# A transformer block with adaptive norm and FP4 quantisers on one core: the scaling of q, two quantiser steps and the row statistics change engine or form, and every order is written anew

## The chip, the cores and the metric

The kernel runs on one core of one Trainium2 chip. The metric is the device time of one execution in microseconds (us). A core has TensorE (PE in the profile; PEld is its weight load), VectorE (DVE), ScalarE (ACT), GpSimd (POOL) and SyncE (SP), which here only issues DMAs. Each engine works through its own list of instructions in order, and the engines wait for each other by semaphores.

## What is computed

There are 32 batches of 256 tokens with 128 features, all float32. Cut to what matters:

```
mod = silu(c) @ wmod                     # six vectors per batch: sa, ca, ga, sb, cb, gb
h = layernorm(x) * (1 + ca) + sa
q, k, v = h @ Wq + bq, ...               # each reshaped to (16 heads, 8, 256)
attn = softmax(k^T v * temperature)      # per head 256 x 256, over the last axis
x = x + ga * (q @ attn)
h = layernorm(x) * (1 + cb) + sb
hid = silu(fp4(h) @ fp4(w_gate).T) * (fp4(h) @ fp4(w_up).T)      # 352 wide
x = x + gb * (fp4(hid) @ fp4(w_down).T)
```

`fp4` quantises blocks of 16 elements: the block's largest magnitude over 6 is the scale, the scaled values are rounded to the grid 0, 0.5, 1, 1.5, 2, 3, 4, 6 and scaled back. With two rows of tokens on each partition, a batch's `h` is 128 x 256 and its `hid` 128 x 704.

## The kernel before

The work is a software pipeline over the batches. Each engine has a function `step(k)` that is called once per step; it names tasks with a lag, and `at(k, 3, maxes, 7)` means that in step k the engine does part 7 of the task `maxes` for batch k - 3. So the order on each engine is written out by hand, task by task, and one step of every engine finishes one batch.

One batch passes through these tasks. `stats1` and `var1` (VectorE: two `bn_stats`, one for each row, two `bn_aggr`, then a variance plus epsilon and a negated mean), `rstd1_pow` and `normalise1` (GpSimd), `x_transpose` (TensorE), `h_out` (ScalarE), `kv_proj` and `q_proj` (TensorE). `k_hi`, `v_hi`, `k_lo`, `v_lo` (VectorE) split k and v into two parts for the fast matmul format; SyncE stores the parts to `split_dram` (`store_split`, eight DMAs a batch) and loads them back in another layout (`load_stacks`, five DMAs). `scores` (TensorE) writes one head's scores into one of the four slots of `score_ps`; `maxes` (VectorE, eight a batch) reads two heads at a time; `exps` (ScalarE, 32 a batch) writes `probs` and the row sums. `row_sums_inv` (VectorE) inverts the sums, `q_out` (ScalarE) copies q out of PSUM into `q_T`, and `q_scaled` (GpSimd) multiplies it by the inverses into `q_z`. `mix` (TensorE) contracts q with the probabilities, `gate1` (VectorE) makes `gated`, `residual1` (GpSimd) makes `x1`.

Then comes the second norm, in the same form as the first (`stats2` to `shift2`), and the two quantisers, of `h2` and of `hid`. Each is: `max`, `scale`, `recip` (VectorE), `y` (GpSimd: value times the reciprocal scale), `exponent` and `magic` (VectorE), `add`, `sub`, `rescale` (GpSimd). `magic` turns the exponent of a value into the number that, added and taken away again, rounds it:

```
def magic(mag):
    return nc.vector.tensor_scalar(mag[:, :], mag[:, :], 1.5, MAGIC, ALU.max, ALU.mult)
```

Between the quantisers stand `gate_proj`, `up_proj`, `tanh`, `silu` and `times_up`, behind them `hid_transpose`, `hidT_out`, `down_proj`, `gate2` (VectorE, makes `ffn_g`), `residual2` and the store. The weights are quantised once, in one piece of 1120 columns, by `ff_weights_max` and `ff_weights_magic` (VectorE), `ff_weights_scaled` and `ff_weights_rounded` (GpSimd), in steps 2 and 3.

Four further PSUM banks are shared by the matmul outputs; `wait_bank` holds a matmul until the readers of the bank's last contents are done.

Of the kernel before, what the change touches and what calls it, by code (L numbers as in the profile page):

```python
# [15 lines left out]
FF = 352  # L16
# [12 lines left out]
STAGES = 10  # L29
# [3 lines left out]
def adaln_block(nc, x, wq, bq, wk, bk, wv, bv, temperature, w_gate, w_up, w_down, c, wmod, out):  # L33
    with ExitStack() as ctx:
# [11 lines left out]
        w_q = sb("w_q", [128, D])  # L46
        w_kv = sb("w_kv", [128, 2, D])
# [4 lines left out]
        minus_half = sb("minus_half", [128, 2])  # L52
# [25 lines left out]
        hT = sb("hT", [128, T])  # L78
# [53 lines left out]
        qT_ps_made, qT_made = sem("qT_ps_made"), sem("qT_made")  # L132
# [15 lines left out]
        ff_zeroed, ff_fp4 = sem("ff_zeroed"), sem("ff_fp4")  # L148
        ff_ps_made, ff_T_made = sem("ff_ps_made"), sem("ff_T_made")
# [43 lines left out]

        @block.sync
        def _(sp):
            sp.dma_start(c_rows[:, :], c).then_inc(c_in, 16)
            sp.dma_start(w_mod[:, :], wmod).then_inc(wmod_in, 16)
# [6 lines left out]
            def load_later():  # L204
# [4 lines left out]
            def load_ff():  # L209
                for i, w in enumerate((w_gate, w_up)):  # L210
                    for t, n in enumerate(FT):
                        sp.dma_start(w_ff[0:n, (3 * i + t) * D:(3 * i + t + 1) * D],
                                     w[128 * t:128 * t + n, :]).then_inc(ff_rows_in, 16)
                sp.dma_start(w_ff[:, 6 * D:NW], w_down).then_inc(ff_rows_in, 16)

            def load_mod(b, c):
                if b == 0:
                    sp.wait_ge(mod_step, 6)
                    sp.dma_start(mod_dram, mod_rows[:, :, :].rearrange("b n f -> b (n f)"))\
                        .then_inc(mod_stored, 16)  # L220
                    sp.wait_ge(mod_stored, 16)
# [28 lines left out]
            def load_stacks(b, c):  # L250
                p = c % 2
                if b < 2:
                    sp.wait_ge(k_zeroed[b], 1)
                wait_dma(sp, split_stored, b, STORES * 16)
                wait_batches(sp, scored, b - 1, H)
                sp.dma_start(v_stack[p][:, :, :].bitcast(F32),
                             split_dram[p, 1].rearrange("g r s j n -> (r s j) g n")).then_inc(stack_loaded[p], 16)
                for r in range(R):
# [32 lines left out]
        def _(pool):  # L291
# [134 lines left out]
            def step(k):  # L426
# [17 lines left out]
                if k == 1:  # L444
                    zero_q()
# [611 lines left out]
```

## Time and profile before

| what | value |
|---|---|
| median of 3 runs | 664.52 us (663.1 to 665.88) |
| the profiled execution's own time | 663.56 us |
| its span, first to last instruction | 661.8 us |
| mean granted TensorE clock | 0.949 of full speed |
| DVE busy | 589.0 us (89%) |
| ACT busy | 566.7 us (86%) |
| PE busy | 550.2 us (83%) |
| POOL busy | 515.0 us (78%) |

The busy shares are means over three parts: a start in which the first batches fill the pipeline, a long even part, and a drain of the last batches. The profiled execution's time stands 1.8 us above its span; that is what lies around the instructions.

### The profile page before, as it was taken

The numbers are of one execution on the slowest core, as the hardware profiler recorded it, in microseconds if no ns is written. First come the engines' busy times: TensorE is split into PE (matmuls) and PEld (weight loads), VectorE is DVE, ScalarE is ACT, GpSimd is POOL, SyncE is SP. The second block draws the span as 40 slices with busy tenths as digits, with TensorE's granted clock in tenths as the row PEclk, the third lists the DMA queues.
The fourth block names the chain that finished last, engine by engine and source line by source line (L and its number), as shares of the span: only waits on it lengthen the run. The fifth ranks groups of instructions, "written<-read, shape, count | busy, mean of one in ns | idle before, by whom it ended". The sixth has DMA issues, their size and how long they took to land.

```text
span 661.8 us, 15572 instructions
## 1 busy us (share of the span) xinstructions
PE 550.2 (83%) x4336; PEld 372.4 (56%) x4336; DVE 589.0 (89%) x1331; ACT 566.7 (86%) x2281; POOL 515.0 (78%) x655
## 2 busy tenths in 40 slices
PE   4468688889999988888888898998888999987773
PEld 2345365666665665566666665665566666654343
DVE  5578489999999999999999999999999999998551
ACT  2289599999999999999999999999999999999111
POOL 2105747888888898988888888888888888877884
PEclk9568799999999999999999999999999999999866
DMA  4656525555566555566555566554556655550000
GB/s 117 160 139 152 137 73 152 136 135 135 156 160 160 136 140 132 141 161 157 145 145 143 145 161 160 151 145 134 141 135 160 160 140 135 136 144 9 10 8 25
DMA packets 87873, 86.14 MB, mean 130 GB/s; under 512 B 8550, under 2 KB 83532, under 8 KB 87788
## 3 DMA queue, kind: packets, MB, share of 16 engines
q1 hardware_dynamic: 87344, 84.94, 49.6%
q8 instruction: 37, 0.61, 0.4%
q14 instruction: 48, 0.39, 0.2%
q10 hardware_dynamic: 444, 0.20, 0.1%
HBM read 47.29 MB, written 37.81 MB: 129 GB/s over the span
## 4 chain that ended last, share of the span: by engine, by line
POOL 36%; DVE 27%; issue 19%; PE 8%; ACT 4%; DMA 2%; SPq 2%; POOLq 1%; DVEq 1%; ACTq 1%
DVE neg_max L638 8%; POOL hid_q L400 7%; POOL hid_q L404 6%; POOL rstd L322 4%; POOL h_c L329 4%; DVE hid L753 3%; DVE hid_am L604 3%; POOL h_c L335 3%; POOL h L342 3%; POOL q_z L355 3%; ACT probs L491 3%; PE bank L935 3%; POOL h_q L375 2%; DVE stats L704 2%; PE score_ps L893 2%
## 5 line engine op out<-in xcount | busy, mean ns | idle before, releaser
L491 ACT ACTIVATE probs<-score_ps,neg_max 128x256 f32<-128x256 f32 x1024 | 472.8, 491 | 22.3 <-DVE neg_max L638 19.8
L638 DVE TENSOR_REDUCE neg_max<-score_ps 128x4 f32<-128x1024 f32 x256 | 308.2, 1204 | 16.5 <-PE score_ps L893 15.9
L893 PE MATMUL score_ps<-v_stack,k_stack 128*128 128x256 f32 x1024 | 212.1, 324 | 48.4 <-DMA k_stack<-split_dram 30.6
L491 ACT ACTIVATION_READ_ACCUMULATOR probs<-score_ps,neg_max 128x1 f32 x1024 | 228.6, 223 | 0.0
L893 PEld LDWEIGHTS score_ps<-v_stack,k_stack 128*128 128x128 f32 x1024 | 148.7, 194 | 118.6 <-ACT probs L491 65.6
L935 PE MATMUL bank<-probs,q_z 128*32 128x256 f32 x2048 | 140.0, 393 | 12.3 <-POOL q_z L355 12.3
L935 PEld LDWEIGHTS bank<-probs,q_z 128*32 128x32 f32 x2048 | 54.5, 111 | 66.9 <-POOL q_z L355 29.9
L955 PE MATMUL bank<-wgu_T,h_T 128*128 128x352 f32 x128 | 52.6, 495 | 18.0 <-issue 17.9
L984 PE MATMUL bank<-wd_T,hid_T 118*128 118x128 f32 x384 | 58.0, 290 | 5.9 <-ACT hid_T L525 5.6
L984 PEld LDWEIGHTS bank<-wd_T,hid_T 118*128 118x128 f32 x384 | 50.4, 199 | 11.7 <-ACT hid_T L525 11.0
L404 POOL TENSOR_TENSOR hid_q<-hid_q,hid_mag 128x704 f32<-128x704 f32 x32 | 53.9, 1685 | 2.5
L400 POOL TENSOR_TENSOR hid_q<-hid_q,hid_mag 128x704 f32<-128x704 f32 x32 | 54.0, 1686 | 2.4 <-DVE hid_mag L615 2.4
L309 POOL TENSOR_TENSOR rstd<-ve,minus_half 128x2 f32<-128x2 f32 x32 | 23.5, 736 | 41.2 <-DVE nm L659 21.9
L525 ACT ACTIVATE hid_T<-bank 118x384 f32<-118x384 f32 x64 | 34.1, 534 | 22.1 <-PE bank L975 21.9
L322 POOL TENSOR_TENSOR rstd<-ve,minus_half 128x2 f32<-128x2 f32 x32 | 30.7, 959 | 28.0 <-DVE nm L718 26.3
L964 PE MATMUL bank<-wgu_T,h_T 128*128 128x352 f32 x128 | 50.5, 482 | 0.5 <-DVE kv_lo L683 0.5
L363 POOL TENSOR_TENSOR x<-gated,x_in 128x256 f32<-128x256 f32 x32 | 23.3, 727 | 30.0 <-DVE gated L696 29.9
L382 POOL TENSOR_TENSOR hid_q<-hid,hid_rs 128x704 f32<-128x704 f32 x32 | 44.5, 1390 | 1.5 <-DVE hid_rs L769 1.3
L409 POOL TENSOR_TENSOR hid_q<-hid_q,hid_sc 128x704 f32<-128x704 f32 x32 | 44.4, 1388 | 0.2
L913 PE MATMUL bank<-w_kv,hT 128*128 128x256 f32 x128 | 41.4, 417 | 1.3 <-ACT hT L501 1.3
L519 ACT ACTIVATE tanh_g<-bank 128x352 f32<-128x352 f32 x64 | 30.2, 472 | 14.0 <-PE bank L955 13.0
L355 POOL TENSOR_TENSOR q_z<-q_T,inv_sum 128x128 f32<-128x128 f32 x64 | 25.1, 415 | 21.1 <-DVE inv_sum L690 21.1
(104 smaller groups left out, 904.0 us busy)
## 6 DMA issues: line engine op xcount, KB each, us to landing
split_dram<-kv_hi SPq DMA_DIRECT2D x128, 128.0 KB, 2.4
split_dram<-kv_lo SPq DMA_DIRECT2D x128, 128.0 KB, 2.4
v_stack<-split_dram SPq DMA_DIRECT2D x32, 512.0 KB, 4.2
k_stack<-split_dram SPq DMA_DIRECT2D x128, 128.0 KB, 4.6
mod_bc<-mod_dram SPq DMA_DIRECT2D x32, 256.0 KB, 5.1
x_in<-in_L_attn_x_dram SPq DMA_DIRECT2D x32, 128.0 KB, 2.5
out_dram<-out_t SPq DMA_DIRECT2D x32, 128.0 KB, 2.1
w_mod<-in_L_wmod_dram SPq DMA_DIRECT2D x1, 384.0 KB, 4.0
```

What stands on the lines that cost most here:

```text
L322: nc.gpsimd.tensor_tensor(rstd2[:, :], ve2[:, :], minus_half[:, :], ALU.pow).then_inc(rstd2_made, 1)
L355: nc.gpsimd.tensor_tensor(dst, q_T[:, c, a, :].rearrange("p (g r j) -> p g r j", g=G, r=R), inv_sum[:, :, a].rearrange("p (g r) -> p g r", ...
L382: nc.gpsimd.tensor_tensor(blocks16(hid_q[:, :], 2 * FF), blocks16(hid[:, :], 2 * FF), spread16(hid_rs[:, :], 2 * FF), ALU.mult).then_inc(h ...
L400: nc.gpsimd.tensor_tensor(hid_q[:, :], hid_q[:, :], hid_mag[:, :], ALU.add).then_inc(hid_t_made, 1)
L404: nc.gpsimd.tensor_tensor(hid_q[:, :], hid_q[:, :], hid_mag[:, :], ALU.subtract)\
L491: nc.scalar.activation(probs[p][:, h, a, :], score_ps[:, h % 4, a, :], ACT.Exp, bias=neg_max[:, p, n:n + 1], accum_out=row_sum[:, p, h, a: ...
L638: nc.vector.tensor_reduce(neg_max[:, p, 4 * u:4 * u + 4], score_ps[:, lo:lo + 2, :, :].rearrange("p b a n -> p (b a) n"), AX.X, ALU.max, n ...
L893: last = nc.tensor.matmul(score_ps[:, h % 4, a, :], k_stack[p][:, h, 128 * a:128 * a + 128], v_stack[p][:, h // R, :], start=True, stop=True)
L935: last = nc.tensor.matmul(bank_mix[32 * g:32 * g + 32, 0:T], q_z[p][:, a, g, r, :], probs[p][:, R * g + r, a, :], start=(i == 0), stop=(i ...
L955: nc.tensor.matmul(bank_gate[a][:, 0:FF], h2_T[:, 128 * a:128 * a + 128], wgu_T[:, 0, :], start=True, stop=True).then_inc(gate_ps_made[a], 1)
L964: nc.tensor.matmul(bank_up[a][:, 0:FF], h2_T[:, 128 * a:128 * a + 128], wgu_T[:, 1, :], start=True, stop=True).then_inc(up_ps_made[a], 1)
L984: last = nc.tensor.matmul(bank_down[:, a * D:(a + 1) * D], hid_T[:, a, t, :], wd_T[:, t, :], start=(t == 0), stop=(t == HT - 1))
```

## The change

On VectorE, `q_scaled` now reads q straight from its PSUM bank, so `q_out` and the tile `q_T` are gone, and `q_proj` moves to the step of the mixing. The row statistics take both rows in one `bn_stats` over interleaved elements; the constant for epsilon stands ready in the tile, a small `tensor_reduce` adds the pairs, another negates the means, and the factor that this form leaves is folded into `mod_T` and `mod_rows`. On GpSimd, `scale` and `magic` of both quantisers are added and `q_scaled` is gone. The weights are quantised in three pieces. ScalarE's queue takes part of the first two batches' stores and loads. `hT` has four buffers, the banks are shared out anew, and all five orders are new (with 14 instead of 10 stages, since the lags are counted in another way).

```diff
-        bank_xT, bank_kv, bank_q, bank_h2T, bank_mix, bank_down = bank_1, bank_3, bank_0, bank_0, bank_2, bank_1
-        bank_gate, bank_up, bank_hidT = (bank_2, bank_1), (bank_3, bank_0), (bank_0, bank_2)
+        bank_xT, bank_kv, bank_q, bank_h2T, bank_mix, bank_down = bank_0, bank_0, bank_2, bank_3, bank_2, bank_1
+        bank_gate, bank_up, bank_hidT = (bank_2, bank_3), (bank_0, bank_3), (bank_0, bank_2)
...
     # gpsimd
-            def q_scaled(b, c):
...
+            def block_scale(sc, am, tiny):
+                return nc.gpsimd.tensor_scalar(sc, am, NUDGE / 6.0, tiny, ALU.mult, ALU.max)
...
+            def magic(mag):
+                return nc.gpsimd.tensor_scalar(mag[:, :], mag[:, :], 1.5, MAGIC, ALU.max, ALU.mult)
+
+            def h2_magic(b, c):
+                pool.wait_ge(h2_z_made, b + 1)
+                magic(h2_mag).then_inc(h2_mag_made, 1)
...
     # scalar
-            def q_out(b, c):
-                wait_batches(act, qT_ps_made, b + 1)
-                wait_batches(act, qz_made, b - 3, 2)
-                nc.scalar.activation(q_T[:, c, :, :], halves(bank_q[:, 0:T]), ACT.Copy).then_inc(qT_made, 1)
...
     # vector
+            def variance(var, stats, p):
+
+                full = stats[:, p, 2:6]
+                pairs = bass.AP(tensor=full.tensor, offset=full.offset, ap=[list(full.ap[0]), [3, 2], [4, 2]])
+                return nc.vector.tensor_reduce(var[:, :], pairs, AX.X, ALU.add)
+
+            def minus_mean(nm, stats, p):
+                return nc.vector.tensor_reduce(nm[:, :], stats[:, p, 1:6:3].unsqueeze(2), AX.X, ALU.max, negate=True)
...
-                for a in range(2):
-                    nc.vector.bn_stats(stats1[:, a, :], x_in[:, b % NX, a, :]).then_inc(stat_a, 1)
...
+                nc.vector.bn_stats(stats1[:, c % 2, 0:6], by_row(x_in[:, b % NX, :, :])).then_inc(stats1_made, 1)
...
+            def q_scaled(b, c):
...
+                for a in range(2):
+                    dst = diagonal(q_z[p][:, a, :, :, :].rearrange("p g r j -> p g (r j)"))
+                    last = nc.vector.tensor_tensor(
+                        dst, bank_q[:, a * 128:(a + 1) * 128].rearrange("p (g r j) -> p g r j", g=G, r=R),
+                        inv_sum[:, :, a].rearrange("p (g r) -> p g r", g=G).unsqueeze(3)
+                        .to_broadcast([128, G, R, DH]), ALU.mult)
...
     # tensor
             def q_proj(b, c):
                 wait_batches(pe, hT_made, b + 1)
-                wait_bank(b, [(h2T_made, b - 3)], (hidT_made[0], b - 5), (hid_made[1], b - 4), (qT_made, b))
+                wait_bank(b, [(silu_made[0], b - 1)], (hidT_made[1], b - 3), (gated_made, b), (qz_made, b))
...
-                at(k, 1, q_proj)
+                at(k, 6, q_proj)
```

Three places of the new orders follow; in each row stand the line, the operation and the tiles.

VectorE, one piece of a step in the even part, from the score maximum ahead of the second norm's statistics to the next maximum. Before:

```order
L638 TENSOR_REDUCE neg_max<-score_ps 128x4
L704 BN_STATS stats<-x 128x6 x2
L666 TENSOR_SCALAR kv_hi<-bank,temp 128x256
L711 BN_AGGR mv<-stats 128x2 x2
L611 TENSOR_SCALAR hid_mag<-hid_q 128x704
L717 TENSOR_SCALAR ve<-mv 128x2
L718 TENSOR_SCALAR nm<-mv 128x2
L615 TENSOR_SCALAR hid_mag<-hid_mag 128x704
L638 TENSOR_REDUCE neg_max<-score_ps 128x4
```

And now:

```order
L753 TENSOR_REDUCE neg_max<-score_ps 128x4
L838 BN_STATS stats<-x 128x6
L761 TENSOR_REDUCE var<-stats 128x2
L764 TENSOR_REDUCE nm<-stats 128x2
L761 TENSOR_REDUCE var<-stats 128x2
L764 TENSOR_REDUCE nm<-stats 128x2
L753 TENSOR_REDUCE neg_max<-score_ps 128x4
```

The two norms' small steps stand together, the split of k has moved behind the next maximum with `exponent` of `hid`, and `magic` has left the engine.

GpSimd, the piece of a step from the first residual to the last step of the quantiser of `hid`. Before:

```order
L363 TENSOR_TENSOR x<-gated,x_in 128x256
L382 TENSOR_TENSOR hid_q<-hid,hid_rs 128x704
L322 TENSOR_TENSOR rstd<-ve,minus_half 128x2
L329 TENSOR_SCALAR h_c<-x,nm,rstd 128x128 x2
L335 TENSOR_TENSOR h_c<-h_c,mod_bc 128x256
L342 TENSOR_TENSOR h<-h_c,mod_bc 128x256
L400 TENSOR_TENSOR hid_q<-hid_q,hid_mag 128x704
L404 TENSOR_TENSOR hid_q<-hid_q,hid_mag 128x704
L355 TENSOR_TENSOR q_z<-q_T,inv_sum 128x4x4x8 x2
```

And now:

```order
L401 TENSOR_TENSOR x<-gated,x_in 128x256
L437 TENSOR_TENSOR hid_q<-hid,hid_rs 128x704
L373 TENSOR_TENSOR rstd<-var,minus_half 128x2
L380 TENSOR_SCALAR h_c<-x,nm,rstd 128x128 x2
L387 TENSOR_TENSOR h_c<-h_c,mod_bc 128x256
L441 TENSOR_SCALAR hid_mag<-hid_mag 128x704
L394 TENSOR_TENSOR h<-h_c,mod_bc 128x256
L466 TENSOR_TENSOR hid_q<-hid_q,hid_mag 128x704
L411 TENSOR_SCALAR h_sc<-h_am 128x16
L470 TENSOR_TENSOR hid_q<-hid_q,hid_mag 128x704
L430 TENSOR_TENSOR h_q<-h,h_rs 128x256
L475 TENSOR_TENSOR hid_q<-hid_q,hid_sc 128x704
```

`magic` of `hid` and `scale` of `h2` (L411) have come in between steps that were neighbours, and the scaling of q is gone; `magic` of `h2` and `scale` of `hid` stand a little further on.

SyncE's queue for the first batch's split parts and their loads. Before:

```order
L229 DMA split_dram<-kv_hi 16x8x256 x2
L229 DMA split_dram<-kv_lo 16x8x256 x2
L229 DMA split_dram<-kv_hi 16x8x256 x2
L201 DMA x_in<-in_L_attn_x_dram 128x256
L229 DMA split_dram<-kv_lo 16x8x256 x2
L256 DMA v_stack<-split_dram 128x4x256
L260 DMA k_stack<-split_dram 32x4x256 x4
```

And now:

```order
L205 DMA split_dram<-kv_hi 16x8x256 x2
L205 DMA split_dram<-kv_lo 16x8x256 x2
L230 DMA v_stack<-split_dram 128x4x256
L240 DMA k_stack<-split_dram 32x4x256 x2
L251 DMA x_in<-in_L_attn_x_dram 128x256
```

The other four stores and two loads stand in ScalarE's queue, and the load of x has moved behind.

## Rows read from the trace of the kernel before

**Rows 1.** The page: its span, and its busy time by engine

```profile
span 661.8 us, 15572 instructions
...
PE 550.2 (83%) x4336; PEld 372.4 (56%) x4336; DVE 589.0 (89%) x1331; ACT 566.7 (86%) x2281; POOL 515.0 (78%) x655
```

**Rows 2.** Windows: busy us of each engine in a stretch of the even part

```profile
core 0: us, PE busy (x) PEld busy (x) DVE busy (x) ACT busy (x) POOL busy (x), PEclk, DMA share, GB/s
...
200.00:300.00 100.00, 90.02 (x770) 61.08 (x770) 98.76 (x228) 97.53 (x397) 87.55 (x113) 1.00 0.57 150
```

**Rows 3.** Timeline of DVE: `gated` of the first, second and last batch

```profile
59.65 0.41 DVE L696 TENSOR_TENSOR gated<-bank,mod_bc 128x256 f32<-128x256 f32 x1
...
83.00 0.41 DVE L696 TENSOR_TENSOR gated<-bank,mod_bc 128x256 f32<-128x256 f32 x1
...
621.22 0.42 DVE L696 TENSOR_TENSOR gated<-bank,mod_bc 128x256 f32<-128x256 f32 x1 [0.92 <-PE bank L935]
```

**Rows 4.** Groups of DVE by form: busy us, mean ns of one, idle before

```profile
L604 DVE TENSOR_REDUCE hid_am<-hid 128x44 f32<-128x704 f32 x32 | 28.0, 874 | 0.3
...
L615 DVE TENSOR_SCALAR hid_mag<-hid_mag 128x704 f32<-128x704 f32 x32 | 16.6, 520 | 0.1
...
L645 DVE BATCH_NORM_STATS2 stats<-x_in 128x6 f32<-128x128 f32 x64 | 15.2, 278 | 0.0
...
L604 DVE TENSOR_REDUCE h_am<-h 128x16 f32<-128x256 f32 x32 | 13.4, 419 | 11.3 <-POOL h L342 10.8
L696 DVE TENSOR_TENSOR gated<-bank,mod_bc 128x256 f32<-128x256 f32 x32 | 13.4, 418 | 0.9 <-PE bank L935 0.9
...
L615 DVE TENSOR_SCALAR h_mag<-h_mag 128x256 f32<-128x256 f32 x32 | 9.2, 287 | 0.2
...
L608 DVE TENSOR_SCALAR h_sc<-h_am 128x16 f32<-128x16 f32 x32 | 8.0, 250 | 0.0
...
L652 DVE BATCH_NORM_AGGREGATE mv<-stats 128x2 f32<-128x6 f32 x64 | 7.6, 160 | 0.0
...
L608 DVE TENSOR_SCALAR hid_sc<-hid_am 128x44 f32<-128x44 f32 x32 | 6.4, 200 | 0.1
...
L658 DVE TENSOR_SCALAR ve<-mv 128x2 f32<-128x2 f32 x32 | 6.2, 195 | 0.0
```

**Rows 5.** Timeline of DVE in the even part: start us, us, instruction

```profile
249.15 0.52 DVE L615 TENSOR_SCALAR hid_mag<-hid_mag 128x704 f32<-128x704 f32 x1
249.59 1.21 DVE L638 TENSOR_REDUCE neg_max<-score_ps 128x4 f32<-128x1024 f32 x1
```

**Rows 6.** Groups of POOL and ACT by form: busy us, mean ns of one

```profile
L400 POOL TENSOR_TENSOR hid_q<-hid_q,hid_mag 128x704 f32<-128x704 f32 x32 | 54.0, 1686 | 2.4 <-DVE hid_mag L615 2.4
...
L316 POOL TENSOR_SCALAR xn<-x_in,nm,rstd 128x128 f32<-128x128 f32 x64 | 28.9, 462 | 0.4
...
L355 POOL TENSOR_TENSOR q_z<-q_T,inv_sum 128x128 f32<-128x128 f32 x64 | 25.1, 415 | 21.1 <-DVE inv_sum L690 21.1
...
L507 ACT ACTIVATE q_T<-bank 128x256 f32<-128x256 f32 x32 | 12.7, 395 | 16.3 <-PE bank L926 16.2
...
L297 POOL MEMSET b_pad<- 128x384 f32 x1 | 0.4, 418 | 0.0
```

**Rows 7.** Timeline near the end: `h_sc` on DVE beside a POOL instruction

```profile
612.02 1.68 POOL L400 TENSOR_TENSOR hid_q<-hid_q,hid_mag 128x704 f32<-128x704 f32 x1
...
612.76 0.96 DVE L608 TENSOR_SCALAR h_sc<-h_am 128x16 f32<-128x16 f32 x1
```

**Rows 8.** Timeline of DVE at the start: first score maximum, and a long wait

```profile
29.15 1.22 DVE L638 TENSOR_REDUCE neg_max<-score_ps 128x4 f32<-128x1024 f32 x1 [6.78 <-PE score_ps L893]
...
77.53 0.29 DVE L611 TENSOR_SCALAR h_mag<-h_q 128x256 int32<-128x256 int32 x1 [7.64 <-POOL h_q L375]
```

**Rows 9.** Timeline of SP's queue: first batch's first stores, last loads

```profile
13.40 1.20 SPq L229 DMA_DIRECT2D split_dram<-kv_hi  x2
...
21.37 1.93 SPq L260 DMA_DIRECT2D k_stack<-split_dram  x4
```

More of the change, by code:

```diff
@@ L1 @@
+import math
 from contextlib import ExitStack
@@ L21 @@
 NW = 2 * 3 * D + FF
+FFC = (slice(0, 3 * D), slice(3 * D, 6 * D), slice(6 * D, NW))
+FFB = tuple(slice(s.start // QB, s.stop // QB) for s in FFC)
 EPS = 1e-5
@@ L250, in load_stacks @@
-            def load_stacks(b, c):
[L251 to L258, printed above, removed]
-                    rows = slice(32 * r, 32 * r + 32)
-                    sp.dma_start(k_stack[p][rows, r:H:R, :].bitcast(F32),
-                                 split_dram[p, 0, :, r].rearrange("g s j n -> (s j) g n"))\
-                        .then_inc(stack_loaded[p], 16)
+                if b >= 2:
+                    store_v_hi_on(sp, b, c)
@@ L483, in exps, with store_v_hi, store_v_lo, load_k_stack @@
+            def store_v_hi(b, c):
+                if b < 2:
+                    store_v_hi_on(act, b, c)
+            def store_v_lo(b, c):
+                if b < 2:
+                    store_v_lo_on(act, b, c)
+            def load_k_stack(b, c):
+                if b < 2:
+                    for r in range(R // 2, R):
+                        load_k_stack_on(act, b, c, r)
             def exps(b, c, h):
@@ L593, in gates @@
                 nc.vector.tensor_copy(mod_rows[:, 1, :], rows[:, 1, :]).then_inc(mod_step, 1)
-                nc.vector.tensor_scalar(mod_rows[:, 2, :], rows[:, 2, :], 1.0, None, ALU.add).then_inc(mod_step, 1)
+                nc.vector.tensor_scalar(mod_rows[:, 2, :], rows[:, 2, :], 1.0, ROOT_D, ALU.add, ALU.mult).then_inc(mod_step, 1)
                 dve.wait_ge(mod_step, 4)
@@ new lines, in step @@
+                at(k, 10, hid_recip)
+                at(k, 7, maxes, 5)
+                if k == 5:
+                    ff_recip(0)
+                at(k, 8, stats2_rows)
+                at(k, 8, variance2)
+                at(k, 4, variance1)
+                if k == 6:
+                    ff_recip(2)
+                at(k, 7, maxes, 6)
+                at(k, 5, v_hi)
+                at(k, 5, k_hi)
+                if k == 3:
+                    ff_recip(1)
+                at(k, 10, hid_exponent)
@@ new lines, in step @@
+                at(k, 7, maxes, 7)
+                at(k, 5, v_lo)
+                at(k, 5, k_lo)
+                at(k, 9, silu, 0)
+                at(k, 6, maxes, 0)
+                if k == 4:
+                    shift_and_scale()
+                at(k, 8, h2_max)
+                if k == 4:
+                    biases()
+                at(k, 7, row_sums_inv)
+                at(k, 9, silu, 1)
+                at(k, 8, h2_recip)
+                at(k, 6, maxes, 1)
+                if k == 6:
+                    ff_exponent(0)
@@ new lines, in step @@
+                if k == 5:
+                    zero_k(0)
+                if k == 4:
+                    ff_exponent(1)
+                at(k, 7, q_scaled)
+                if k == 6:
+                    ff_exponent(2)
+                if k == 5:
+                    ff_magic(1)
+                if k == 4:
+                    ff_max(0)
+                if k == 5:
+                    ff_max(2)
+                if k == 0:
+                    ff_max(1)
+                at(k, 9, times_up, 0)
```

732 lines of the change are left out of this document (395 added, 337 removed).

## The prediction

> **What bounds the kernel now.** I read the page's busy line first, then a stretch of the even part, then single starts.
>
> The busy line [rows 1] only says that four engines are close: DVE 589.0, ACT 566.7, PE 550.2, POOL 515.0 of a span of 661.8 us. The stretch [rows 2] says more: in 100 us DVE works 98.76, ACT 97.53, PE 90.02, POOL 87.55. So VectorE sets the pace there, ScalarE stands just behind it, and GpSimd has slack.
>
> The pace itself comes from the starts of `gated` [rows 3]: second batch 83.00, last 621.22, so 538.22 us for 30 steps, 17.94 us a step. In one step DVE works 17.72 and waits 0.22, ACT works 17.50, POOL 15.71. What is not in those 30 steps is the start, 83.0 us to the second `gated`, and the drain, 661.8 - 621.2 = 40.6 us behind the last. All sums below are 30 steps plus what start and drain change.
>
> A duration is not what an instruction costs DVE, since the next one starts before it ends: `magic` of `hid` lasts 0.52 and the next starts 0.44 behind it [rows 5]. I take 0.08 us off each duration.
>
> **DVE, part by part, for one step.** Removed [rows 4]: four `bn_stats` of 128 elements (two rows of each norm; the second norm's group reads the same), 4 x (0.278 - 0.08) = 0.79. Four `bn_aggr`, 4 x 0.08 = 0.32. Four additions and negations of the mean, priced like `ve` at 0.195, 4 x 0.115 = 0.46; the trace shows most of them shorter, so I take 0.36. `scale` twice, 0.17 + 0.12 = 0.29. `magic` twice, 0.44 + 0.21 = 0.65. Together 2.41.
>
> Added: two `bn_stats` of 256. VectorE's reductions give a slope, (874 - 419) / 448 = 1.02 ns an element, so 128 more elements cost 0.13 and one costs 0.33, two 0.66. Four tiny `tensor_reduce`: the same line at nearly no elements gives 0.16, less 0.08, so 0.32. Two multiplications of q from PSUM: `gated` also reads PSUM, 0.418 for 256, so 0.29 for 128, less 0.08, and 0.42 for both. Together 1.40. Bounds for what the trace doesn't show: the interleaved `bn_stats` may cost as little as today's (0.40 for two) or the whole duration of two today's each (1.11); the split pattern of q may cost up to the whole 0.418 of `gated` twice (0.84). I take the slope, as the operations are the nearest kinds. Net: -1.01, with ends -1.27 and -0.14. DVE's work becomes 16.7.
>
> DVE also has waits. It keeps 0.22, and the two `exponent` steps, which remain, can be held by GpSimd: `h_sc` takes 0.96 instead of some 0.16 while a POOL instruction of 1.68 runs beside it, and both end at 613.7 [rows 7]. Before, ten such scalar operations a step met a GpSimd that was idle 12% of the time; now two meet one that hardly idles. I put 0.3 on it, so DVE asks for about 17.2.
>
> This is also what the Trainium skill states, SBUF — State Buffer, Who interferes with whom: VectorE in a two-port mode and GpSimd take one pair of ports as an exclusive lock, and the loser waits out the whole instruction. By that rule, the trace agrees (0.96 for a 128x16 operation), and it speaks against loading GpSimd further.
>
> **ACT.** `q_out` goes, 0.395 long [rows 6]; its neighbours overlap it, so I count two thirds, 0.26 a step, with ends 0 and 0.395. 17.50 becomes 17.2, and some of the 17.50 is waiting for maxima that the busy time hides.
>
> **GpSimd.** `q_scaled` goes, 2 x 0.415 = 0.83 [rows 6]. Two `magic` and two `scale` come. The trace has no such operation at that size. The low end is a memset's 1.09 ns an element all in: 0.77 and 0.28. The high end is the nearest operation, `xn`, 0.462 for 128 elements, taken as proportional: 2.54 and 0.92. In between lies a two-input operation, 1.69 for 704 and, on the line through 0.415 for 128, 0.70 for 256. I take `xn` for the first 128 elements and the memset's slope for the rest, since `magic` reads one tile like `xn`: 1.09 and 0.60. The two `scale` are below `xn`, 0.25 each. Sum: 15.71 - 0.83 + 1.69 + 0.50 = 17.07, and 0.2 for neighbours that wait for each other. So GpSimd asks for 17.3.
>
> The Trainium skill, GPSIMD Engine Reference, 4.1 Engine selection, calls GpSimd about half as fast as VectorE with two inputs, but roughly at line rate with one. By the first part `magic` would cost 1.69 and 0.70 and the gain of the even part would be gone; by the second it is close to the value I took. No row of this trace decides.
>
> Three engines then ask for 17.2, 17.2 and 17.3 in a step. None has slack to give another. The new order also asks for short answers: `scale` of `h2` stands on GpSimd between `add` and `sub` of `hid`, and VectorE has only an inversion and a `silu` between `max` and `recip` to cover it, so a late GpSimd shows at once as a wait of DVE. I take the longest, **17.3**: 30 x (17.3 - 17.94) = **-19.2**.
>
> **The start.** First scores: SP issues eight stores and five loads for the first batch between 13.40 and 23.30 [rows 9]. Half of the stores and two loads go to the other queue, and a load of x moves behind. Four stores at 0.6, two loads at 0.48 and the x load at 0.6 make 3.96, so the first maximum comes at about 25 instead of 29.15 [rows 8]. The new work ahead (a memset of `k_stack` now behind the split, weights in thirds) lies beside DMAs in flight. Bounds: 0, if ScalarE's queue is late by what SyncE's gains, and 5. Weights: the second `gated` comes 23.35 behind the first, 5.4 more than a step, and DVE waits 7.64 us at 77.53 for `h_q`, which stood behind the whole weight work on GpSimd [rows 3, 8]. In three pieces spread over steps with no FFN work I leave 1.4 of it, so -4.0 (ends 0 and -5.4). Start: **-8**, from 0 to -10.
>
> **The drain.** Behind the last `gated`, GpSimd takes three `hid` and one `h2` through the quantisers. For each `hid`, `magic` costs 1.09 instead of 0.52 and `scale` 0.05 more: +0.6 for two, in a chain; for the first, where GpSimd never idles, +1.3. **+2.5**, from 0 to +5.
>
> **Sum**, against the profiled execution's 663.6 (0.96 below the median of the runs shown): 663.6 - 19.2 - 8 + 2.5 = 638.9, **639**.
>
> **The rivals.**
> - *The start only.* The even part keeps its pace, 17.9: the ring of maximum, exponentials and the next scores in `score_ps`, or one of the banks (x, kv, up and hid now share one), waits longer than DVE gains. For it: ACT is at 97.53 already. Against it: `maxes` is not made longer and ACT loses 0.26. -1.2 - 8 + 2.5 gives 657. Chance 0.10.
> - *The held exponents.* Each waits half an average POOL instruction (515.0 us over 655 is 0.79 [rows 1]), 0.4 instead of 0.15: 16.7 + 0.22 + 0.8 makes DVE ask for 17.75. -5.7 - 8 + 2.5 gives 652. Chance 0.10.
> - *GpSimd at the price of two inputs.* 15.71 - 0.83 + 2.39 + 0.5 + 0.2 = 18.0 a step: +1.8 - 8 + 4 gives 661, no change. Against it: the memset's row. Chance 0.08.
> - *Slower: GpSimd becomes the bound.* `magic` at the proportional price, 2.54 + 0.92: 15.71 - 0.83 + 3.46 + 0.5 + 0.2 = 19.0. 30 x 1.1 = 33, - 8 + 5, gives 693. It decides from 18.15 a step on, since start and drain give back 3 us and 3.3 must be lost. Chance 0.10.
> - *My forecast*, 626 to 651. Chance 0.62.
>
> **How the numbers follow.** 0.5%, 3.3 us, is about what a measurement of this kernel tells from no change. The forecast's own range: at 17.0 a step, -28 - 10 + 0 gives 626; at 17.55, -11.7 - 4 + 3 gives 651. With the next two rivals at 652 and 657 it reaches 658 and holds 0.82. Faster: 0.62 + 0.10 + 0.10 = 0.82. Same: 0.08. Slower: 0.10.
>
> **What would show it.** In the profile after: `gated` at steps of 17.3, first maximum at 25, the second `gated` some 8 earlier than 83; DVE near 16.7 and POOL near 17 busy a step; `magic` on GpSimd 1.1 and 0.6; `bn_stats` 0.41; `exponent` of `hid` at most 0.3 longer than now on average. Wrong would be: `magic` above 1.7, DVE and POOL both with slack while the step stays near 17.9 (then the ring or a bank), or a first maximum later than 29.

## The result: slower by 7%, GpSimd sets the pace

The changed kernel took 712.15 us (median of 4 runs, 709.68 to 713.79) against 665.20 for the kernel before (663.1 to 668.83): a ratio of 1.0697, 95% interval 1.0639 to 1.0754. The forecast was 639, with 693 for the rival in which GpSimd becomes the bound. Its profiled execution has a span of 710.8 us.

The page of the changed kernel, its span, its busy time, and the shares of the engines in its chain of waits:

```profile
span 710.8 us, 15569 instructions
...
PE 556.7 (78%) x4336; PEld 380.9 (54%) x4336; DVE 567.8 (80%) x1084; ACT 559.8 (79%) x2249; POOL 625.3 (88%) x730
...
POOL 72%; issue 16%; ACT 4%; PE 3%; DVE 2%; DMA 2%; POOLq 1%; SPq 1%; ACTq 0%
```

The same stretch as in [rows 2], and `gated` of the second and the last batch as in [rows 3]:

```profile
200.00:300.00 100.00, 81.71 (x675) 56.90 (x675) 85.17 (x166) 86.72 (x350) 95.94 (x111) 1.00 0.48 132
```

```profile
72.10 0.41 DVE L830 TENSOR_TENSOR gated<-bank,mod_bc 128x256 f32<-128x256 f32 x1
...
662.83 0.42 DVE L830 TENSOR_TENSOR gated<-bank,mod_bc 128x256 f32<-128x256 f32 x1 [2.02 <-PE bank L1063]
```

The busy share has changed sides: GpSimd from 87.55 to 95.94, VectorE from 98.76 to 85.17. The step is (662.83 - 72.10) / 30 = 19.69 us, not 17.94: +52.5 over 30 steps. The second `gated` comes 10.9 earlier than 83.00, and the drain is 710.8 - 662.8 = 48.0 instead of 40.6, +7.4. Together +49.0, which is what the spans differ by.

The groups of GpSimd and VectorE that answer to [rows 4] and [rows 6] (mean ns of one behind the busy time; then the idle time before them and what ended it):

```profile
L441 POOL TENSOR_SCALAR hid_mag<-hid_mag 128x704 f32<-128x704 f32 x32 | 82.4, 2576 | 5.9 <-DVE hid_mag L723 3.7
L466 POOL TENSOR_TENSOR hid_q<-hid_q,hid_mag 128x704 f32<-128x704 f32 x32 | 53.8, 1680 | 0.2
...
L441 POOL TENSOR_SCALAR h_mag<-h_mag 128x256 f32<-128x256 f32 x32 | 34.6, 1081 | 5.5 <-DVE h_mag L723 3.3
L366 POOL TENSOR_SCALAR xn<-x_in,nm,rstd 128x128 f32<-128x128 f32 x64 | 28.2, 448 | 3.2
...
L411 POOL TENSOR_SCALAR hid_sc<-hid_am 128x44 f32<-128x44 f32 x32 | 11.8, 368 | 3.0 <-DVE hid_am L720 0.3
L411 POOL TENSOR_SCALAR h_sc<-h_am 128x16 f32<-128x16 f32 x32 | 8.9, 279 | 8.1 <-DVE h_am L720 5.4
```

```profile
L723 DVE TENSOR_SCALAR hid_mag<-hid_q 128x704 int32<-128x704 int32 x32 | 19.0, 593 | 4.5 <-POOL hid_q L437 4.5
...
L820 DVE TENSOR_TENSOR q_z<-bank,inv_sum 128x128 f32<-128x128 f32 x64 | 15.1, 277 | 0.0
...
L720 DVE TENSOR_REDUCE h_am<-h 128x16 f32<-128x256 f32 x32 | 13.4, 419 | 30.6 <-POOL h L394 30.6
L769 DVE BATCH_NORM_STATS2 stats<-x_in 128x6 f32<-128x256 f32 x32 | 13.4, 419 | 0.0
...
L761 DVE TENSOR_REDUCE var<-stats 128x2 f32<-128x4 f32 x64 | 9.2, 152 | 1.4 <-issue 0.2
...
L856 DVE RECIPROCAL h_rs<-h_sc 128x16 f32<-128x16 f32 x32 | 8.1, 253 | 28.9 <-POOL h_sc L411 28.9
```

One line matters most: `magic` of `hid` takes 2.58 us on GpSimd, more than `add` or `sub` with their two inputs (1.68) and five times its 0.52 on VectorE. What VectorE saved has become waiting for GpSimd: 28.9 us ahead of `h_rs` and 30.6 ahead of `h_am` (where it was 11.3 before), about 0.9 us a step each. The added VectorE operations last as long as the forecast said.

GpSimd itself hardly waits for anyone. In some 15 steps from 200 us on it pauses nine times a step, 0.08 to 0.11 us each, and only two of the 133 pauses are longer (0.48). Part of its busy time is holding by VectorE all the same: the two `normalise2` instructions take 1.25 us together where they took 0.89 before, with VectorE's `exponent` of `hid` beside the second.

```profile
271.47 1.25 POOL L380 TENSOR_SCALAR h_c<-x,nm,rstd 128x128 f32<-128x128 f32 x2
```

```profile
271.96 0.52 DVE L723 TENSOR_SCALAR hid_mag<-hid_q 128x704 int32<-128x704 int32 x1
```

In the kernel before, the `rstd` ahead of them was the one that was long, 0.97 us instead of 0.71 beside `magic` of `hid`. So only 0.1 us a step of this is new.

### The profile page after: what moved, and what is told of

Same layout as the page of the kernel before. It is cut to its first block, busy times and chain, and to the rows that moved or that the text cites. A ratio compares the mean times of both kernels' runs of the same rounds, so it can differ in the third digit from the quotient of the medians.

```text
span 710.8 us, 15569 instructions
## 1 busy us (share of the span) xinstructions
PE 556.7 (78%) x4336; PEld 380.9 (54%) x4336; DVE 567.8 (80%) x1084; ACT 559.8 (79%) x2249; POOL 625.3 (88%) x730
## 4 chain that ended last, share of the span: by engine, by line
POOL 72%; issue 16%; ACT 4%; PE 3%; DVE 2%; DMA 2%; POOLq 1%; SPq 1%; ACTq 0%
POOL hid_mag L441 12%; POOL hid_q L466 8%; POOL hid_q L470 8%; POOL hid_q L475 6%; POOL h_c L380 5%; POOL h_mag L441 5%; POOL hid_q L437 4%; ACT probs L604 3%; POOL xn L366 3%; POOL rstd L373 3%; POOL h_q L453 3%; POOL h_c L387 3%; POOL h_q L457 3%; POOL x L401 3%; POOL rstd L359 2%
## 5 line engine op out<-in xcount | busy, mean ns | idle before, releaser
L753 DVE TENSOR_REDUCE neg_max<-score_ps 128x4 f32<-128x1024 f32 x256 | 308.5, 1206 | 17.8 <-PE score_ps L1019 17.3
L1019 PE MATMUL score_ps<-v_stack,k_stack 128*128 128x256 f32 x1024 | 230.5, 327 | 44.0 <-ACT probs L604 39.3
L1019 PEld LDWEIGHTS score_ps<-v_stack,k_stack 128*128 128x128 f32 x1024 | 154.8, 194 | 135.5 <-ACT probs L604 90.0
L1063 PE MATMUL bank<-probs,q_z 128*32 128x256 f32 x2048 | 137.6, 400 | 44.1 <-DVE q_z L820 44.1
L1063 PEld LDWEIGHTS bank<-probs,q_z 128*32 128x32 f32 x2048 | 62.9, 113 | 86.9 <-DVE q_z L820 49.6
L441 POOL TENSOR_SCALAR hid_mag<-hid_mag 128x704 f32<-128x704 f32 x32 | 82.4, 2576 | 5.9 <-DVE hid_mag L723 3.7
L633 ACT ACTIVATE hid_T<-bank 118x384 f32<-118x384 f32 x64 | 32.4, 508 | 40.9 <-PE bank L1109 40.6
L1097 PE MATMUL bank<-wgu_T,h_T 128*128 128x352 f32 x128 | 51.0, 480 | 16.7 <-issue 16.7
L1109 PE MATMUL bank<-ident,hid_q 128*118 128x128 f32 x192 | 33.2, 286 | 16.2 <-POOL hid_q L475 15.6
L441 POOL TENSOR_SCALAR h_mag<-h_mag 128x256 f32<-128x256 f32 x32 | 34.6, 1081 | 5.5 <-DVE h_mag L723 3.3
L380 POOL TENSOR_SCALAR h_c<-x,nm,rstd 128x128 f32<-128x128 f32 x64 | 35.8, 567 | 3.5
L720 DVE TENSOR_REDUCE h_am<-h 128x16 f32<-128x256 f32 x32 | 13.4, 419 | 30.6 <-POOL h L394 30.6
```

What stands on the lines that cost most here:

```text
L380: nc.gpsimd.tensor_scalar(h2_c[:, a, :], x1[:, c, a, :], nm2[:, a:a + 1], rstd2[:, a:a + 1], ALU.add, ALU.mult).then_inc(h2_c_made, 1)
L441: return nc.gpsimd.tensor_scalar(mag[:, :], mag[:, :], 1.5, MAGIC, ALU.max, ALU.mult)
L753: nc.vector.tensor_reduce(neg_max[:, p, 4 * u:4 * u + 4], score_ps[:, lo:lo + 2, :, :].rearrange("p b a n -> p (b a) n"), AX.X, ALU.max, n ...
L1019: last = nc.tensor.matmul(score_ps[:, h % 4, a, :], k_stack[p][:, h, 128 * a:128 * a + 128], v_stack[p][:, h // R, :], start=True, stop=True)
L1063: last = nc.tensor.matmul(bank_mix[32 * g:32 * g + 32, 0:T], q_z[p][:, a, g, r, :], probs[p][:, R * g + r, a, :], start=(i == 0), stop=(i ...
L1097: nc.tensor.matmul(bank_up[a][:, 0:FF], h2_T[:, 128 * a:128 * a + 128], wgu_T[:, 1, :], start=True, stop=True).then_inc(up_ps_made[a], 1)
```

## The experiments

Each time has the kernel before beside it on the same chip, and the ratio is to that; steps are worked out from `gated` as above. A and B are the two theories that each expectation weighs. From the fifth run on, the base is the changed kernel with a cheap `magic` (run 5); run 7 is the kernel before with it, and runs 9 and 11 are edits of run 6.

A step is the mean over 30, and some steps near both ends are shorter than the rest. Between 200 and 500 us it is (492.45 - 210.11) / 16 = 17.65 us in run 5 where the mean is 17.49, and 17.98 before, 19.99 in the change, 18.92 in run 6, 18.30 in run 8, 17.56 in run 10 and 18.64 in run 11. Below, this is the even step, and it goes with busy shares of 200 to 500 us.

### 1. Both magics back on VectorE, all else as changed

```diff
-                at(k, 9, h2_magic)          # gpsimd
-                at(k, 10, hid_magic)
+                at(k, 9, h2_magic)          # vector, behind h2_exponent
+                at(k, 10, hid_magic)        # vector, behind hid_exponent
```

> The changed kernel with both magic steps back on VectorE, each right behind its exponent; all else as changed. Theory A (the price of magic on GpSimd, 2.58 + 1.08 us a step, is what made the step 19.7 us): GpSimd falls from about 19.7 to 16.0 a step, VectorE asks for 16.9 + 0.65 = 17.5 and sets the pace, step about 17.6; with start 72 and drain about 41 the run takes about 643 us. Rival B (the new orders, the shared banks or the handshakes of scale between the two engines cost it): the step stays at 18.5 or more and the run takes over 670 us.

Measured: 680.68 us (679.27 to 682.94), ratio 1.0229 [1.0193, 1.0266], step 18.86. Moving the magics back returns 31 of the 47 us, and GpSimd's busy share falls to 82% (200 to 500 us), but A's 643 did not come. The numbers are B's: a step of 18.5 or more, over 670 us. They don't show B's reason, since run 5 keeps the same orders, banks and scales and has a step of 17.49. VectorE is 97.6% busy here, and two of its groups show where part of the time went:

```profile
L713 DVE TENSOR_SCALAR hid_mag<-hid_q 128x704 int32<-128x704 int32 x32 | 28.3, 883 | 4.5 <-POOL hid_q L437 4.5
L717 DVE TENSOR_SCALAR hid_mag<-hid_mag 128x704 f32<-128x704 f32 x32 | 28.1, 879 | 1.1
```

`exponent` and `magic` of `hid` take 0.88 each instead of 0.50 and 0.52. In all steps from 200 to 500 us each of them begins beside a GpSimd instruction and ends 0.37 to 0.39 us behind that one's end. Runs 6, 9 and 11 look at this.

### 2. The kernel before, both magics on GpSimd alone

```diff
-                at(k, 4, h2_magic)          # vector
-                at(k, 6, hid_magic)
+                at(k, 4, h2_magic)          # gpsimd, ahead of h2_add
+                at(k, 5, hid_magic)         # gpsimd, ahead of hid_add
```

> The kernel before with one part of the change alone: both magic steps on GpSimd, ahead of their add; its own orders, banks and statistics stay. Theory A: GpSimd asks for 15.7 + 3.66 = 19.4 and some gaps, step 19.6 to 20.2, run 715 to 735 us, slower than the whole change. Rival B (the orders are the cost): the slack of GpSimd takes most of it and the run stays below 690 us.

Measured: 785.66 us (784.65 to 788.71), ratio 1.1798 [1.1756, 1.1841], step 21.86. Worse than both theories. The magics take 2.56 and 1.07 here too, but GpSimd is only 86% busy from 200 to 500 us. The waits point to its answers coming too late in the old order: TensorE's weight loads wait 103 us for `q_z`, and VectorE 95 us for `h_q`. TensorE's granted clock is 0.92 in this stretch, where it was 1.00 before, so part of the length may be TensorE's; no run separates this.

### 3. A multiplication in place of the maximum

```diff
-                return nc.gpsimd.tensor_scalar(mag[:, :], mag[:, :], 1.5, MAGIC, ALU.max, ALU.mult)
+                return nc.gpsimd.tensor_scalar(mag[:, :], mag[:, :], 1.5, MAGIC, ALU.mult, ALU.mult)
```

> The changed kernel with a multiplication in place of the maximum in magic on GpSimd (the rounding numbers come out otherwise, the work is the same). If the maximum is the dear operation: magic of hid takes 1.0 to 1.3 us instead of 2.58 and the step falls to about 18. If every operation with one input and two constants costs that: it stays at 2.58, and the run at about 712 us.

This version leaves out the floor of `magic`, so its rounding numbers and its output are wrong, and only its time is of use. Measured, one run: 635.89 us, step (592.1 - 70.3) / 30 = 17.39. One operation in each of the two magics moves the time by 76 us. The magics take 0.78 and 0.41, below the 1.0 to 1.3 that was expected of a cheap one.

### 4. GpSimd's price list

A kernel of its own that computes nothing of the block: GpSimd is the only engine that computes, and runs each form four times over 44, 128, 256 and 704 elements.

```diff
+ run(lambda: nc.gpsimd.tensor_scalar(tiles[name][:, 0:n], src[:, 0:n], 1.5, 2.0, op0, op1))
+ run(lambda: nc.gpsimd.tensor_scalar(tiles[name][:, 0:n], src[:, 0:n], 1.5, None, op0))
+ run(lambda: nc.gpsimd.tensor_scalar(tiles[name][:, 0:n], src[:, 0:n], sc[:, 0:1], sc[:, 1:2], op0, ALU.mult))
```

> Only the price list: GpSimd runs one-input operations on 44, 128, 256 and 704 elements, each waiting for the one ahead, with nothing beside it; no reference work is done and the output is zeros. Line rate (theory of my prediction): any one-input form takes about 0.2 + 0.83 ns an element, 0.8 to 1.1 us for 704. Dear maximum: forms with max take about 2.58 for 704 and 1.08 for 256, add and mult forms less than half of it. Dear second operation: two operations cost about twice one.

Measured; the groups by form, six at 704 elements and two at 128 (the tile's name is the form):

```profile
L73 POOL TENSOR_SCALAR max_mult<-src 128x704 f32<-128x704 f32 x4 | 10.2, 2558 | 0.4
...
L75 POOL TENSOR_SCALAR max_only<-src 128x704 f32<-128x704 f32 x4 | 7.9, 1972 | 0.3
L79 POOL TENSOR_TENSOR tt_add<-src 128x704 f32<-128x704 f32 x4 | 5.4, 1357 | 0.3
...
L77 POOL TENSOR_SCALAR add_mult_ptr<-src,sc 128x704 f32<-128x704 f32 x4 | 3.7, 930 | 0.4
...
L73 POOL TENSOR_SCALAR add_mult<-src 128x704 f32<-128x704 f32 x4 | 3.1, 777 | 0.3
L80 POOL COPY copy<-src 128x704 f32<-128x704 f32 x4 | 3.1, 769 | 0.3
...
L73 POOL TENSOR_SCALAR max_mult<-src 128x128 f32<-128x128 f32 x4 | 2.5, 637 | 0.4
...
L77 POOL TENSOR_SCALAR add_mult_ptr<-src,sc 128x128 f32<-128x128 f32 x4 | 1.8, 449 | 0.4
```

Two additions or multiplications cost as much as a copy. A maximum among the two makes it 3.3 times as much. No other engine computes, and SyncE's stores of the output are over long before the 704-element instructions start at 74 us, so no contention is in it. The theory that two operations cost twice one has fallen too: a single operation (1.97) is dearer than two multiplications (0.78). The form of `xn` (`add_mult_ptr`) is 0.449 at 128 elements, near the 0.462 of [rows 6], and 0.930 at 704.

### 5. The same rounding numbers by multiply and add

The maximum only has to keep the number from falling below 1.5 x 2^22. With 15/32 x 2^22 times the exponent's 1.5 x 2^e, plus 1.25 x 2^22, the number lies in the same power of two for all exponents that occur.

```diff
-                return nc.gpsimd.tensor_scalar(mag[:, :], mag[:, :], 1.5, MAGIC, ALU.max, ALU.mult)
+                return nc.gpsimd.tensor_scalar(mag[:, :], mag[:, :], MAGIC * 15 / 32, MAGIC * 1.25, ALU.mult, ALU.add)
```

> The changed kernel with the magic numbers on GpSimd made by multiply and add in place of maximum and multiply: the exponent's 1.5 x 2^e times 15/32 x 2^22, plus 1.25 x 2^22. That lies in the same power of two as the old number for every exponent that occurs and is a whole, even multiple of its last place, so all values that are rounded come out as before. A (the maximum's price on GpSimd is the whole of what went wrong): magic 0.78 and 0.41 us as with two multiplications, step of gated 17.4, time 633 to 640, 4 to 5% below the kernel before. B (it was the rounding numbers of the run with two multiplications, not the price, that made that run short): 700 or more.

Measured: 639.36 us (638.3 to 642.04), ratio 0.9596 [0.9568, 0.9624]: 4% below the kernel before and 10% below the change. Its stretch, and the magic's group:

```profile
200.00:300.00 100.00, 91.61 (x786) 63.63 (x786) 95.48 (x186) 95.97 (x399) 95.06 (x126) 1.00 0.59 155
```

```profile
L441 POOL TENSOR_SCALAR hid_mag<-hid_mag 128x704 f32<-128x704 f32 x32 | 24.9, 778 | 4.7 <-DVE hid_mag L723 2.2
```

The step is (595.2 - 70.5) / 30 = 17.49. GpSimd is 95.0% busy over 200 to 500 us, much as with the dear `magic` (95.7%), so 0.86 to 0.88 us of each even step are idle on it in both, whatever its work. A's numbers came (magic 0.78 and 0.41, 633 to 640 us).

### 6. The scales back on VectorE

```diff
+                at(k, 8, h2_scale)          # vector, behind row_sums_inv
+                at(k, 10, hid_scale)        # vector, behind maxes 4
```

> As the run with multiply and add, but with both scales of h2 and hid moved back to VectorE. GpSimd loses 0.37 + 0.28 = 0.65 us a step, VectorE gains 0.17 + 0.12 by the rows of before, some 0.5 if GpSimd holds the ports. A (GpSimd and the handshake over it set the pace, as they did at 19.69): the step falls by 0.2 to 0.5, time 620 to 630. B (with the cheap magic VectorE and GpSimd ask for the same time, so that the move only changes who is late): 634 to 645.

Measured: 669.27 us (668.13 to 671.38), ratio 1.0043 [1.002, 1.0066], step 18.58. Both theories missed: two operations of 16 and 44 elements a partition cost 30 us. The group of `h_sc`, then its place in the timeline of VectorE and what GpSimd does beside it:

```profile
L842 DVE TENSOR_SCALAR h_sc<-h_am 128x16 f32<-128x16 f32 x32 | 33.3, 1039 | 0.0
```

```profile
319.98 1.18 DVE L842 TENSOR_SCALAR h_sc<-h_am 128x16 f32<-128x16 f32 x1
```

```profile
319.45 1.68 POOL L460 TENSOR_TENSOR hid_q<-hid_q,hid_mag 128x704 f32<-128x704 f32 x1
```

`h_sc` ends at 321.16, `sub` of `hid` at 321.13. The orders are regular: in all 16 steps from 200 to 500 us `h_sc` begins 0.5 us behind the start of `sub`, takes 1.18 to 1.20 and ends 0.02 to 0.04 behind its end. In the first two steps, with no GpSimd instruction beside it, it takes 0.12. Over the whole run `hid_sc` takes 0.55, and `exponent` of `hid` 0.84 instead of 0.55. VectorE is 99.4% busy: 18.80 us of an even step instead of 16.82. Of these 2.0 us more it had 0.8 to spare, which leaves 1.2 to 1.3, and the even step is 18.92 - 17.65 = 1.27 longer.

### 7. The kernel before with the cheap magic on GpSimd

The edit of run 2 with the operation of run 5.

```diff
+                return nc.gpsimd.tensor_scalar(mag[:, :], mag[:, :], MAGIC * 15 / 32, MAGIC * 1.25, ALU.mult, ALU.add)
```

> The kernel before in its old orders, with only the two magics moved to GpSimd, in the cheap form. GpSimd gets 1.19 us a step more (15.71 to 16.9), VectorE loses 0.65. A (the orders do not matter, only the sums): the step goes from 17.94 to some 17.6, time 650 to 657. B (the old order has GpSimd's answers in a chain in which VectorE waits; with the dear magic it took 21.86 us a step, and the cheap one gives back 2.47 of it): 700 to 715.

Measured: 698.26 us (697.83 to 699.4), ratio 1.0475 [1.0445, 1.0506], step 19.00. Just below B's 700 to 715, but B's chain is at most part of it, for VectorE is 97.0% busy (200 to 500 us). The scales, still on VectorE here, are held again: 0.98 and 0.50 instead of 0.25 and 0.20. In the kernel before, `h_sc` meets only the last 0.09 us of `add` and is done when `sub` starts:

```profile
308.32 0.16 DVE L608 TENSOR_SCALAR h_sc<-h_am 128x16 f32<-128x16 f32 x1
```

```profile
306.72 1.69 POOL L400 TENSOR_TENSOR hid_q<-hid_q,hid_mag 128x704 f32<-128x704 f32 x1
...
308.49 1.69 POOL L404 TENSOR_TENSOR hid_q<-hid_q,hid_mag 128x704 f32<-128x704 f32 x1
```

With `magic` ahead of them GpSimd's instructions shift. `h_sc` now begins 0.6 us behind the start of `add`, takes 1.1 us in the even part, and ends with it:

```profile
319.89 1.67 POOL L411 TENSOR_TENSOR hid_q<-hid_q,hid_mag 128x704 f32<-128x704 f32 x1
...
320.50 1.10 DVE L621 TENSOR_SCALAR h_sc<-h_am 128x16 f32<-128x16 f32 x1
```

### 8. Only the magic of h2 by maximum

```diff
-                magic(h2_mag).then_inc(h2_mag_made, 1)
+                nc.gpsimd.tensor_scalar(h2_mag[:, :], h2_mag[:, :], 1.5, MAGIC, ALU.max, ALU.mult)\
+                    .then_inc(h2_mag_made, 1)
```

> As the run with multiply and add, but with the magic of h2 alone by maximum and multiply, which adds 0.66 us to GpSimd's step. GpSimd works some 16.6 of 17.4 us in the version with two multiplications. A (GpSimd sets the pace, us for us, as from 17.39 to 19.69 for 2.47 us added): step +0.6, time 651 to 657. B (GpSimd has 0.8 us a step to spare and takes this in): 636 to 645.

Measured: 658.64 us (658.25 to 659.49), ratio 0.988 [0.9851, 0.9909], step 18.07. 0.68 us more on GpSimd (1.08 instead of 0.41) make the even step 18.30 - 17.65 = 0.65 longer, and the mean step 0.58. From run 5 to the change GpSimd gets 2.47 more, and the steps are 2.34 and 2.20 longer. So it is A's mechanism, close to one for one in the even part; the time lies 1.6 above A's 651 to 657.

### 9. The scales on VectorE in another form

```diff
-                return nc.vector.tensor_scalar(sc, am, NUDGE / 6.0, tiny, ALU.mult, ALU.max)
+                return nc.vector.scalar_tensor_tensor(out=sc, in0=am, scalar=NUDGE / 6.0,
+                                                      in1=tiny.to_broadcast([128, am.shape[1]]),
+                                                      op0=ALU.mult, op1=ALU.max)
```

> As the run with both scales on VectorE (669.3 us, step 18.6), but each written as scalar_tensor_tensor, (am x factor) max a constant tile, in place of tensor_scalar; same place, same values. A (the scales were dear there because VectorE's tensor_scalar is held while a GpSimd instruction runs, 1.04 and 0.55 us for 16 and 44 elements, and the two-input form isn't held): they take 0.15 to 0.25 us, and the time falls to 628 to 645. B (they were dear for their place, or because VectorE has no time left at all): scales still near 1 us, 660 to 672.

Measured: 671.83 us (670.72 to 672.82), ratio 1.0082 [1.0066, 1.0098], step 18.63.

```profile
L845 DVE SCALAR_TENSOR_TENSOR h_sc<-h_am,tinies 128x16 f32<-128x16 f32 x32 | 33.2, 1039 | 0.0
```

To the nanosecond the same, and again it ends 0.02 to 0.04 us behind `sub` in the even part. A's part, that only `tensor_scalar` is held, has fallen: this form, which reads two tiles in SBUF and writes a third, is held too.

### 10. VectorE's statistics twice

```diff
+                nc.vector.bn_stats(spare[:, :], by_row(x_in[:, b % NX, :, :]))
                 nc.vector.bn_stats(stats1[:, c % 2, 0:6], by_row(x_in[:, b % NX, :, :])).then_inc(stats1_made, 1)
```

> As the run with multiply and add (639.4 us, step 17.49), but VectorE computes each of the two row statistics twice, the first time into a spare tile: 2 x 0.35 = 0.7 us more VectorE work a step, nothing for GpSimd or ScalarE. A (VectorE has no slack either, the three engines hang together): step +0.5 to +0.7, 655 to 661. B (GpSimd alone sets the pace, VectorE's idle 4.5% takes it in): 637 to 645.

Measured: 640.72 us (639.13 to 641.53), ratio 0.961 [0.9589, 0.963], step (597.4 - 72.7) / 30 = 17.49, the same as in run 5. The stretch:

```profile
200.00:300.00 100.00, 91.29 (x780) 63.23 (x779) 99.41 (x197) 98.12 (x400) 94.89 (x125) 1.00 0.57 154
```

VectorE takes some 0.6 us more in an even step and goes from 95.5 to 99.4 busy, and the step stays as it is. That is B: the engine with 95% sets the pace, the one with 99% doesn't.

### 11. The scale of h2 one instruction later

```diff
-                at(k, 8, h2_scale)
                 at(k, 9, silu, 1)
+                at(k, 8, h2_scale)
```

> As the run with both scales on VectorE (669.3 us, step 18.58), but the scale of h2 stands one instruction later, behind the second silu. A (it is held until the GpSimd instruction beside it ends, in the timeline hid's subtraction at about 304.6 in both): it starts 0.43 us later and ends at the same moment, so its mean falls from 1.04 to some 0.6 and its step by 0.3 to 0.45: 656 to 661. B (its length is the price of the operation on VectorE, wherever it stands): still 1.04 us and 667 to 672.

Measured: 665.57 us (664.14 to 667.53), against 667.26 for the kernel before, ratio 0.9979 [0.9957, 1.0001]; step 18.44, mean of `h_sc` 0.846.

```profile
320.65 0.82 DVE L842 TENSOR_SCALAR h_sc<-h_am 128x16 f32<-128x16 f32 x1
```

```profile
319.74 1.70 POOL L460 TENSOR_TENSOR hid_q<-hid_q,hid_mag 128x704 f32<-128x704 f32 x1
```

It still ends with `sub`, at 321.47 against 321.44, and is shorter for having started later, so B has fallen. `sub` begins 0.91 ahead of `h_sc` here and 0.53 in run 6, so the two have shifted by 0.38 against each other, and from 200 to 500 us `h_sc` takes 0.82 instead of 1.19, 0.37 less; the means over the whole run, 0.85 and 1.04, blur this. The even step falls by 18.92 - 18.64 = 0.28, near A's 0.3 to 0.45. The mean step falls by 0.14 only, since some steps near both ends are longer than in run 6, and so 665.57 us lies above A's range.

## Why the prediction was wrong

**The step that failed** is the price of `magic`: "I take `xn` for the first 128 elements and the memset's slope for the rest, since `magic` reads one tile like `xn`: 1.09 and 0.60." It measured 2.58 and 1.08. The row was near in shape, in engine and in the kind of instruction, but not in the two arithmetic operations, which decide by a factor of 3.3. For the form of `xn` the working was sound: 0.93 at 704 elements and 0.56 at 256 by run 4. The proportional end, 2.54 and 0.92, which carried the slower rival at a chance of 0.10, came close, above all for `hid`. That was luck, since in run 4 the form of `xn` itself is not proportional.

**The rival.** "GpSimd becomes the bound" named the mechanism and a step of 19.0 and 693 us. It came as 19.69 (19.99 in the even part) and 712. What the step lacked: the idle time that GpSimd keeps, 0.86 us where the sum had 0.2; the magics at 3.66 instead of 3.46; the scales at 0.37 and 0.28 where it had 0.25 each; and some 0.1 by which VectorE holds it more than before. With these 1.1 us the sum comes to 20.15, against the even step's 19.99. The drain was +7.4 instead of +5. The point from which it decides was put at 18.15. Run 8, at 18.07, is still 1.2% below the kernel before, because the start gives back 11.

**VectorE.** Forecast 16.7 us of work a step; in run 5 it is 95.3% of the even step's 17.65, or 16.8. `bn_stats` 0.42 to 0.43 (forecast 0.41), the tiny reductions 0.15 (0.16), q from PSUM 0.277 (0.29). These terms stand. ScalarE's work was forecast at 17.2 and is 17.0. Run 10 adds that VectorE had at least 0.6 us of slack in run 5, and it was idler still in the change, so its sum, however right, was not what the time hung on.

**The held operations.** The forecast put 0.3 on two exponents. In run 5 they are longer by 0.05 and 0.07. The mechanism was right and its size depends on the place, as run 6 shows with 2.0 us for three operations. That moving the scales off VectorE was worth 30 us in this order, the forecast did not see; it priced them at 0.29 a step. Nor did it have a term for GpSimd being held by VectorE, the 0.36 us of `normalise2` above. The Trainium skill, SBUF — State Buffer, Who interferes with whom, has the loser of the ports wait out the whole instruction; the trace agrees, with ends 0.03 us apart in runs 6 and 11.

**Start and drain.** The first maximum came at 27.21, not 25: 1.9 of the 4.0 that the queues were to bring. The second `gated` came 10.9 earlier (12.5 in run 5) instead of 8: the distance from the first to the second `gated` is 17.36 instead of 23.35, so the weights no longer cost anything, where 1.4 had been left for them. These two make 7.9 of the 10.9. The other 3.0 lie between the first maximum and the first `gated`, for which the forecast had no term; TensorE's granted clock has a mean of 0.73 there before and 0.95 now:

```profile
27.00:60.00 33.00, 25.26 (x140) 16.68 (x140) 24.93 (x37) 26.03 (x109) 6.47 (x9) 0.73 0.57 147
```

```profile
27.00:60.00 33.00, 26.63 (x148) 17.64 (x147) 24.57 (x39) 28.64 (x121) 12.14 (x18) 0.95 0.54 140
```

Both means lie between the clock's two levels, 1.2 and 2.4 GHz. No run shows how much of the start is the clock's and how much the new order's. The drain has three magics of `hid` and one of `h2`, 6.1 us dearer in the change than in run 5, where it is 41.4, +0.8.

**The sum without the failed step.** Run 5 is the change with `magic` at 0.78 and 0.41. Its step is 17.49 for a forecast of 17.3, its second `gated` 70.5 for 75, its drain 41.4 for 43.1, and its time 639.36 for 639. That the two agree is partly luck, a longer step against a shorter start. And with these magics the forecast's own sum for GpSimd is 15.71 - 0.83 + 1.19 + 0.50 = 16.57, less than the 17.2 of VectorE and ScalarE. Its work came to 16.8, but its idle time is 0.88 and not 0.2, and so it sets the pace even here. That is a second step that failed, hidden behind the first: the 0.2 for "neighbours that wait for each other".

**What stays open.** What makes the pauses of 0.08 to 0.11 us, nine a step in the change and ten in run 5, that add up to GpSimd's idle time of 0.86 to 0.88. The trace names no cause for pauses this short. And how much of run 1's 18.86 is the held operations and how much is GpSimd waiting for `h_am` behind its `scale` (62 us in all); no run took these apart.

## What to carry to other kernels

Before work moves to another engine, find a row with the same pair of arithmetic operations, not only the same kind and shape, and where there is none, let the far end of the bounds weigh: here it decided everything, and a kernel of one engine would have shown it. A floor or a clamp need not be a maximum: here a multiplication and an addition rounded to the same values at 0.78 instead of 2.58 us. On VectorE, a tiny `tensor_scalar` or `scalar_tensor_tensor` on SBUF lasts as long as the GpSimd instruction that it meets; put it on GpSimd itself or where GpSimd pauses. Read the pace from an experiment, since the busiest engine (99.4%) was not the one that set it.

## What the runs showed of the hardware

- GpSimd's `tensor_scalar` with a maximum as one of its two operations costs (2558 - 1066) / 448 = 3.3 ns an element; with additions and multiplications (779 - 406) / 448 = 0.83. With a single operation, a multiplication as much as a maximum, it is 1.97 us for 704 elements, dearer than with two multiplications. The Trainium skill, GPSIMD Engine Reference, 4.1 Engine selection, has GpSimd roughly at line rate with one input; 0.78 for 704 agrees with this, 2.56 and 1.97 do not, and the measurement decides.
- VectorE's `tensor_scalar` and `scalar_tensor_tensor` from SBUF to SBUF both end with the GpSimd instruction beside them (a mean of 1.04 us for 16 elements in either form, 0.11 to 0.12 with none beside). With 704 elements, `exponent` ends 0.38 us behind it.
- GpSimd is held as well: 0.81 us instead of 0.45 for 128 elements beside VectorE's `exponent` of `hid`, and 0.97 instead of 0.71 for a `pow` of 2 elements beside its `magic`. In run 10 `exponent` falls on the next GpSimd instruction, which then takes 0.96 instead of 0.73, and the one ahead is back at 0.45.
